# Gram of four samples as four matmuls on the four quarters of the array's columns, one unit a tile

## The reference

```python
e = stack([tbl_f[ids[:, f]] for f in range(26)], axis=1)         # 512 x 26 x 128
combined = concatenate([dense[:, None, :], e], axis=1)           # 512 x 27 x 128
inter = einsum('bfd,bgd->bfg', combined, combined)[:, iu, ju]    # the 351 pairs f < g
h = concatenate([dense, inter, dense], axis=1)                   # 512 x 607
h = maximum(h @ W_top1 + b_top1, 0)                              # 512 x 512
h = maximum(h @ W_top2 + b_top2, 0)                              # 512 x 256
y = h @ W_top3                                                   # 512 x 1
```

## Time and profile before

| | |
|---|---|
| median of three runs | 219.22 us (218.92 to 219.71) |
| span of the profiled execution, first to last instruction | 151.2 us |
| what the median has beyond that span | 68.0 us |
| TensorE matmuls busy | 113.5 us, 756 records |
| VectorE busy | 83.7 us, 237 |
| ACT busy | 81.7 us, 251 |
| GpSimd busy | 81.6 us, 89 |

### The profile page before, as it was taken

One profiled execution on the slowest core, in us unless ns is written; L12 is line 12 of the kernel. 1 busy time (PEld: TensorE's weight loads), 2 busy tenths in 40 slices (PEclk: granted clock), 3 DMA queues, 4 the chain that ended last, 5 costly groups with the idle time before them and its releaser, 6 DMA issues.

```text
span 151.2 us, 2296 instructions
## 1 busy us (share of the span) xinstructions
PE 113.5 (75%) x756; PEld 102.3 (68%) x756; DVE 83.7 (55%) x237; ACT 81.7 (54%) x251; POOL 81.6 (54%) x89
## 2 busy tenths in 40 slices
PE   0549940687979948099888999999998979979700
PEld 0337920657849847098787998999888959869500
DVE  3569680626398431719839800797989954860100
ACT  6287550829155999964539953240987424872000
POOL 2777787777787777777777777877700000000000
PEclk9999999999999999959999999999999999999985
DMA  4454479754344823122211222466610000000000
GB/s 96 147 162 157 136 210 230 177 160 139 110 137 136 305 72 81 52 57 58 52 52 52 56 57 58 55 40 54 59 26 4 0 0 0 0 4 0 0 0 0
DMA packets 7088, 12.06 MB, mean 80 GB/s; under 512 B 2970, under 2 KB 4223, under 8 KB 6949
## 3 DMA queue, kind: packets, MB, share of 16 engines
q0 software_dynamic: 2624, 5.38, 18.0%
q1 hardware_dynamic: 3925, 6.28, 13.3%
q10 hardware_dynamic: 528, 0.26, 0.7%
HBM read 10.78 MB, written 0.00 MB: 71 GB/s over the span
## 4 chain that ended last, share of the span: by engine, by line
PE 49%; ACT 18%; DMA 18%; DVE 5%; issue 4%; SPq 0%; ACTq 0%; DVEq 0%
DMA tab<-in_tbl_dram 18%; ACT z L479 14%; PE ps L681 12%; PE ps L719 11%; PE ps L662 6%; PE ps L734 5%; PE ps L645 5%; PE ps L648 5%; PE ps L628 3%; DVE z L567 3%; ACT emb_t L470 2%; DVE tab_lo L515 2%; ACT tab_hi L419 1%; ACT emb_t L449 1%; PE ps L615 1%
## 5 line engine op out<-in xcount | busy, mean ns | idle before, releaser
L404 POOL DMA_INDIRECT rows<-in_tbl_dram,ids_i x82 | 80.8, 986 | 27.4 <-issue 24.7
L479 ACT COPY z<-ps 32x40 f32<-32x40 f32 (+2 forms) x160 | 38.0, 238 | 13.8 <-PE ps L681 11.8
L645 PE MATMUL ps<-hot,tab_hi 125*128 125x256 f32 x88 | 29.3, 355 | 10.6 <-ACT emb_t L449 8.7
L527 DVE TENSOR_SCALAR hot<-ps,row_no 125x256 fp32r<-125x256 f32 x73 | 29.8, 474 | 11.6 <-PE ps L615 11.6
L681 PE MATMUL ps<-emb_t 128*128 128x104 f32 x256 | 31.0, 277 | 6.2 <-ACT z L479 3.1
L681 PEld LDWEIGHTS ps<-emb_t 128*128 128x128 f32 x256 | 29.6, 192 | 7.9 <-ACT z L479 4.3
L645 PEld LDWEIGHTS ps<-hot,tab_hi 125*128 125x128 f32 x88 | 22.0, 250 | 12.0 <-ACT emb_t L449 9.5
L648 PE MATMUL ps<-hot,tab_lo 125*128 125x256 f32 x88 | 28.0, 341 | 0.8 <-DVE tab_lo L515 0.8
L567 DVE COPY z<-ps 32x40 f32<-32x40 f32 (+2 forms) x84 | 19.5, 233 | 9.0 <-PE ps L681 7.7
L648 PEld LDWEIGHTS ps<-hot,tab_lo 125*128 125x128 f32 x88 | 21.9, 249 | 1.4 <-DVE tab_lo L515 1.4
L662 PE MATMUL ps<-ident,rows 128*128 128x128 f32 x82 | 14.7, 305 | 5.1 <-ACT emb_t L470 4.8
(11 more groups left out here) (51 smaller groups left out, 91.8 us busy)
## 6 DMA issues: line engine op xcount, KB each, us to landing
tab<-in_tbl_dram SPq DMA_DIRECT2D x6, 500.0 KB
rows<-in_tbl_dram,ids_i POOLq DMA_INDIRECT x82, 3.8
w_fold<-w_pair SPq DMA_DIRECT2D x1, 1024.0 KB
w<-in_W_top_dram SPq DMA_DIRECT2D x1, 512.0 KB, 15.5
x_rows<-in_r_dense_features_dram ACTq DMA_DIRECT2D x1, 256.0 KB, 3.5
w_x<-in_W_top_dram SPq DMA_DIRECT2D x1, 256.0 KB, 3.9
h_t<-in_W_top_dram SPq DMA_DIRECT2D x1, 256.0 KB, 14.5
w<-in_W_top_dram SPq DMA_DIRECT2D x1, 128.0 KB
```

Source lines behind the costliest of these rows:

```text
L404: pool.indirect_dma_start(out=rows[:, t % 2, gathered.index(f), :], out_offset=None, in_=tables[f - 1], in_offset=bass.IndirectOffsetOnAxi ...
L479: last = nc.scalar.copy(dst, src)
L527: nc.vector.tensor_scalar(hot[0:RP, k % OHB], ps[0:RP, IDV[h] + n % 2, 0:HB], row_no[0:RP, c:c + 1], None, ALU.is_equal).then_inc(hot_dve, 1)
L645: nc.tensor.matmul(bank, tab_hi[0:RP, n, c], one_hot, start=c == 0, stop=False)
```

## The change

A unit becomes a whole tile: `UG` is 32, so a tile has one unit of 128 samples, and `ORDER` has one `u0` a line. In the line of tile 0 the table product that stood between the units `u0-1` and `u2-3` comes after the whole Gram. A call of four samples becomes four calls (`GT = 1`): sample q has a stationary operand of 128 x 32 and a moving one of 128 x 26, and its result goes to partitions 32q to 32q+31 of PSUM. All four blocks now lie in the same 26 columns, so 16 calls' worth of them (`BG`) fit in one bank, and the 128 samples in banks 2 and 3. The copies keep their pattern with 16 groups a bank in place of 4: 16 copies a tile, each of four times as many elements.

```diff
-    "u0-1 h u2-3 g0 h g1 h g2 h g3 h g4-5",
-    "u0-3 g0 h x0 l0:0 l1:0 g1 l2:0 l3:0 g2 e0 g3 d0-2:2 x1 l0:1 l1:1 g4 d3-5:2 l2:1 g5 l3:1 e1",
-    "u0-3 p2 d0-5:3 g0 x2 l0:2 g1 l1:2 g2 l2:2 g3 l3:2 e2 g4 g5",
-    "u0-3 p3 x3 l0-3:3 e3",
+    "u0 h g0 h g1 h g2 h g3 h g4-5",
+    "u0 g0 h x0 l0:0 l1:0 g1 l2:0 l3:0 g2 e0 g3 d0-2:2 x1 l0:1 l1:1 g4 d3-5:2 l2:1 g5 l3:1 e1",
+    "u0 p2 d0-5:3 g0 x2 l0:2 g1 l1:2 g2 l2:2 g3 l3:2 e2 g4 g5",
+    "u0 p3 x3 l0-3:3 e3",
...
-    UG = 8
+    UG = 32
+    GT = 1
     UB = GB * UG
     NU = P // UB
-    GC = GB * NCOL
+    GC = GT * NCOL
     BK = 512
+    BG = UG // 2
+    assert BG * GC <= BK
...
-                    src = ps[32 * q:32 * q + SLOTS, bank:bank + 2, 0:4 * GC].rearrange(
-                        "p k (g c) -> p k g c", g=4)[:, :, :, q * NCOL + r:q * NCOL + cols:4]
+                    own = q % GT * NCOL
+                    src = ps[32 * q:32 * q + SLOTS, bank:bank + 2, 0:BG * GC].rearrange(
+                        "p k (g c) -> p k g c", g=BG)[:, :, :, own + r:own + cols:4]
...
                     for g in range(UG):
-                        b0 = u * UB + g * GB
-                        last = nc.tensor.matmul(ps[:, GRAM + 2 * (u % 2) + g // 4, g % 4 * GC:(g % 4 + 1) * GC],
-                                                emb_t[:, t, b0:b0 + GB, :].rearrange("p b f -> p (b f)"),
-                                                emb_t[:, t, b0:b0 + GB, 0:NCOL], start=True, stop=True)
+                        bank, col = GRAM + 2 * (u % 2) + g // BG, g % BG * GC
+                        for q in range(0, GB, GT):
+                            b0 = u * UB + g * GB + q
+                            last = nc.tensor.matmul(ps[32 * q:32 * (q + GT), bank, col:col + GC],
+                                                    emb_t[:, t, b0:b0 + GT, :].rearrange("p b f -> p (b f)"),
+                                                    emb_t[:, t, b0:b0 + GT, 0:NCOL], start=True, stop=True)
                     last.then_inc(gram_ps, 1)
```

## The result

The changed kernel takes 233.97 us, the median of five runs (232.86 to 238.47), where the kernel before takes 219.22: a ratio of 1.0647 (95% interval 1.0585 to 1.071), slower. The forecast was slower with 225.2 us; the sign and the wide range held, the size did not: +14.75 us where +6.0 was expected. Ratios and their intervals compare only the executions within 1.5% of the fastest of each kernel, medians are of all, so the two differ a little.

A forecast was written before the change was run, and what follows sets the result against it. Bound: ACT's copies in tile 0, Gram matmuls in tiles 2 and 3, tile 1 between. Terms for tiles 0 to 3, 0.5 + 0.6 + 2.45 + 2.4 = +6.0 us, on the 219.22 us median gave 225.2 us; range 209 to 252.

The forecast's parts named there:

- The pair of 32 ns: Price of one small weight load plus matmul in the Gram: 32 ns, range 28 to 38, chance 0.40.
- the 100 ns of the 39 column load: Upper bound on the small pair: the smallest load in TensorE's steady stream came 100 ns before the next.
- the quarters overlap: Rival, 0.26: Gram loads and matmuls of four column quarters run side by side; at 16 ns a pair, -10.4 us, 208.8.
- Each ns on the pair moves the sum by 1.02 us.: All four Grams lie on the path, so each ns of pair price changes the total by 1.02 us.
- A tile's Gram is 8.4 us: Each tile's Gram on TensorE: 256 pairs at 0.032 us, plus 0.2 for the last one's end.
- tile 0's term: Tile 0: ACT saves 7.7 us, eaten by copies starting later and the table product now behind them; net +0.5 us.
- The copies: 16 larger copies a tile: ACT 548, 492 and 436 ns each, VectorE 610, 543 and 475.
- The rival of cheap copies: Rival, 0.07: the copies' element price falls for longer patterns; +0.9 us or less, about 219.8 us.
- Tiles 2 and 3: From Gram start to z ready, 12.5 us instead of 10.0: +2.45 and +2.4 us, with TensorE idle 3 us.
- The clock: Rival, 0.05: granted clock falls to 0.5 in the lightly used Gram; pair 64 ns, +33 us, 252 us.
- Slower: Forecast sign for the whole kernel: slower than before, +6.0 us, with chance 0.67.
- the break-even of 26 ns: Price of a Gram pair at which the forecast sum would be no change.

The follow-up runs named there:

- run 9: The kernel before with the gathers of tiles 1 to 3 left out, every tile transposing tile 0's gathered rows: 154.72 us.
- run 10: The changed kernel with the gathers of tiles 1 to 3 left out, every tile transposing tile 0's gathered rows: 155.0 us.
- run 1: The kernel before, unchanged, measured and profiled again: 218.72 us.
- run 3: The changed kernel with tile 1's gathers held until tile 0's Gram is done, and tile 2's until tile 1's: 219.75 us, ratio 0.9981 to the kernel before.
- run 5: The kernel before with tile 1's gathers held until tile 0's Gram is done, and tile 2's until tile 1's: 225.44 us, ratio 1.0167.
- run 6: The kernel before with four small matmuls per call in tiles 0 and 1 only, old units and copies: 234.41 us, ratio 1.0542.
- run 4: The changed kernel with two samples a call on half the columns and units of 64 samples: 219.49 us, ratio 1.0031 to the kernel before.
- run 8: The kernel before with each large Gram call of tiles 0 and 1 issued twice: 234.06 us, ratio 1.0553.
- run 12: The changed kernel with two samples a call in all tiles and gathers held until the previous tile's Gram is done: 211.52 us, ratio 0.9604 to the kernel before.

## Why the prediction failed in size

**The pair of 32 ns.** The term on which all hung was wrong by a factor of four, to the other side: 8.5 ns. The first step that failed is "I take 32 ns". Its lower bound of 16, from two loads in a row, was not low enough, and the 100 ns of the 39 column load were not the price of a small load; the text suspected the matmul before it, which no run tests. The rival "the quarters overlap", 0.26, was right in its mechanism, not in the gain of 10 us that it gave. The Trainium skill, "TensorE: Matmul & The Clock Gate", Part 3: Packing small matmuls, says matmuls in different column groups run at once; the 8.5 ns agree. The Trainium skill's floor of about 25 ns between starts, same page, Wait — 56ns, not 53.3ns?, which I held against the change, does not hold across the quarters: here a load and a matmul together took 8.5 ns.

**"Each ns on the pair moves the sum by 1.02 us."** By that rule 8.5 ns would give 6.0 - 24.1 = -18 us in a kernel without the gathers' waits. Runs 9 and 10 show no such gain. The rule supposed that TensorE always has its next instruction. Without gathers it stands still after 209 to 238 pairs for 2.0 to 3.2 us, and in tile 3 after 111 to 123 for 3.4 to 4.4, so the Gram lasts 4.6 to 8.9 us where 256 x 8.5 ns are 2.2. Neither sum nor rivals had that wait.

**"A tile's Gram is 8.4 us".** Measured: 30.2, 32.0, 5.1 and 8.2. This is where the size went wrong. The terms of the sum were 0.5, 0.6, 2.45 and 2.4 us for tiles 0 to 3; by the first two lines of the table the changed kernel loses 4.4, 6.2, 1.3 and 3.4. So the terms of tiles 2 and 3 are near as a sum, and those of tiles 0 and 1, 1.1 us together, are 10.6. For these two the step that failed comes before any price: the trace was taken for the execution whose time is to be forecast, and the 68.0 us between its span and the median for something that lies outside and does not change. They were waits inside, while gathers run. Runs 1 and 9 show it (216.7 us span; 154.72 us without gathers). Runs 3, 5 and 6 show that the loss comes from the small matmuls beside the gathers; that it goes by the number of instructions, and not by their shape, rests on the timelines of runs 4 and 8. In a stretch of gathers the kernel before gets its 64 Gram pairs and the next product through. The changed kernel gets 96 of 256 pairs through, and has the other 160, the copies of a whole tile and the product still to do when it ends: layer 1 of tile 0, which stands behind tile 1's Gram, starts 12.8 us after the last gather ended (164.88 and 152.04), for 4.75 in run 1 (151.32 and 146.57). One step of tile 0's term held: the product behind the whole Gram starts 0.67 us after the copies' end (113.76 and 113.09), for 0.65 forecast.

**The copies.** 548, 436 and 475 ns were forecast for the ACT copies of 224 and 160 elements and VectorE's of 160; 562, 434 and 433 were measured. Tile 0's 16 took 8.41 us for 8.5. The rival of cheap copies is out.

**Tiles 2 and 3.** 12.5 us from the Gram to layer 1 was forecast; 8.9 and 11.9 were measured. Tile 3's is near for the wrong reason: pauses for instructions, not the matmuls' own pace. The forecast idle time of 3 us before layer 1 was 2.2 and 2.5.

**The clock.** The rival said the granted clock would be 0.5 in the Gram: in the gathers' time it is 0.53 and 0.56 as the mean of the two Grams' windows (74.4 to 98.6 and 127.8 to 152.1), where TensorE mostly stands still; the pair of 64 ns that the rival foresaw is not there. (Its sum was wrong as well: 64 ns give 6.0 + 32.8 = 38.8 us, so 258 us, not 252.) The clock's small part of the loss is in layer 1 behind: 2.48 and 2.26 us for two blocks of ten that took 1.35 and 1.28, so 2.1 us in tile 2, and 4.22 us for the 20 that took 2.47, 1.75 us in tile 3. A pause does not always bring it: behind the one in tile 2 of run 10 the first ten take 1.35 us.

**Where the sign came from.** "Slower" came true by none of the steps that led to it: the pair was far under the break-even of 26 ns, and what made the kernel slower was not in the sum. It was luck.

## What to carry to other kernels

Put a trace's span beside the timed median before any price is worked out. If they differ by more than a few us, look for an execution whose span fits, as most of what sets the time may be missing from the one you have. Look in the timeline for what TensorE gets through beside a long row of GpSimd gathers, count its instructions there as a scarce thing if it stalls as here, and place dense runs of small matmuls where none is going; two samples a call with the gathers held back gave 4% here, four times the instructions cost 6.5%. And splitting a matmul over column quarters buys array time only as long as instructions arrive: with no gather beside the Gram there was no wait at 29 ns a pair (run 12), and at 8.5 ns with a whole tile in one unit there always was one.

## What the runs showed of the hardware

- Loads and matmuls of fp32 on the four column quarters, 32 stationary and 26 moving columns, start every 8.5 ns a pair; on halves, 64 and 52 columns, every 29 ns (128 in 3.94 us, less the last one's 0.25); on the whole array every 113.5.
- In all timed executions that were looked at, while GpSimd runs a row of 20 indirect gathers, TensorE starts some 80 to 100 pairs in 25 us, the first 41 to 73 at full pace and then one to six every 0.7 us or more, and goes on at full pace 3 to 4 us after the last gather's instruction ended. That holds for 26, 52 and 104 moving columns. ACT and VectorE then wait up to 34 us for signals whose matmuls have long ended ("remote"). What is held up stays open. It does not look like a transfer of instructions, since in tile 1 of the changed kernel none of the queue's packets moves while TensorE is slow, nor when it recovers. Whether it is the signals, the start of instructions or the recording of them no run takes apart: none compares a recorded execution with one that is not, and the kernel before was once recorded with the same gathers and none of it, in a span of 151.2 us.
- Without gathers TensorE pauses 2.0 to 3.2 us after 209 to 238 of the fast pairs (seven Grams of runs "changed", 3 and 10), and 3.4 to 4.4 us after 111 to 123 in tile 3 of the same runs. At the pace of 29 ns it does not (run 12).
- The instruction queue moves one packet of 16 to 17 KB (0.20 MB in 12, 0.13 in 8) for every 128 pairs more, and one lies at each of these ten pauses. That the pauses are the wait for such a packet fits all of this and is not shown: no run changes the transfers alone.
